# Performer attention: each head's product over its own 32 feature rows

## The reference

```python
q_kernel = jnp.exp(h_q + (proj_q - q_stab))         # q_stab = h_q
k_kernel = jnp.exp(h_k + (proj_k - k_stab))
q_prime = nc * (q_kernel + KERNEL_EPS)              # KERNEL_EPS = 1e-4
k_prime = nc * (k_kernel + KERNEL_EPS)
S = S + kt[..., :, None] * vt[..., None, :]         # a scan over the tokens
Z = Z + kt
num = jnp.einsum('bhm,bhmd->bhd', qt, S)            # m = 32 features
den = jnp.einsum('bhm,bhm->bh', qt, Z)
```

## Time and profile before

| | |
|---|---|
| median of 3 runs | 2310.37 us (2308.21 to 2314.17) |
| profiled execution | 2307.16 us, span 2305.4 us |
| PE busy | 2055.2 us, 89% |
| DVE busy | 1951.0 us, 85% |
| ACT busy | 1476.1 us, 64% |
| POOL busy | 948.3 us, 41% |
| mean granted TensorE clock | 0.958 |

### The profile page before, as it was taken

The page is one execution under the profiler, slowest core; times in us unless marked ns, Lnnn a source line. Parts: engine busy times, 40 slices in busy tenths (PEclk is TensorE's granted clock), DMA queues, the critical chain, the costliest instruction groups (busy, mean ns, idle before and its releaser), DMA issues. The chain is left out here.

```text
span 2305.4 us, 41495 instructions
## 1 busy us (share of the span) xinstructions
PE 2055.2 (89%) x12569; PEld 1606.9 (70%) x12569; DVE 1951.0 (85%) x7828; ACT 1476.1 (64%) x3637; POOL 948.3 (41%) x1374
## 2 busy tenths in 40 slices
PE   5879798989999899998999899898999899888677
PEld 3556577656986578766886579775887669767466
DVE  1289797998989898998989899898989989796982
ACT  3546367776676667686577667676677766468341
POOL 3232213554164534544155443544345541443441
PEclk9878889999999999999999999999999999899798
DMA  4000101000100101001100101001010001001000
GB/s 188 1 8 1 35 7 50 1 8 29 56 4 1 35 6 53 1 2 35 42 18 1 35 2 56 4 1 35 13 47 1 1 29 56 31 1 56 1 3 3
DMA packets 29503, 55.03 MB, mean 24 GB/s; under 512 B 2914, under 2 KB 10082, under 8 KB 28642
## 3 DMA queue, kind: packets, MB, share of 16 engines
q1 hardware_dynamic: 29282, 52.37, 7.0%
HBM read 51.31 MB, written 1.05 MB: 23 GB/s over the span
## 5 line engine op out<-in xcount | busy, mean ns | idle before, releaser
L265 DVE MATCH_REPLACE8 top_work<-top_eight,top_work 128x256 f32<-128x256 f32 x1664 | 666.9, 408 | 0.0
L267 DVE MAX8 top_eight<-top_work 128x8 f32<-128x256 f32 x1664 | 616.7, 412 | 0.2
L305 POOL TENSOR_TENSOR top_p<-top_p,top_rest 128x512 f32<-128x512 f32 x192 | 244.4, 1273 | 217.4 <-ACT top_rest L298 217.4
L850 PE MATMUL bank<-workP 128*128 128x256 f32 x1024 | 278.1, 396 | 9.1 <-POOL workP L1012 4.0
L990 ACT ACTIVATE att_pP<-bank,att_tinyP 128x256 f32<-128x256 f32 x512 | 215.2, 476 | 67.2 <-DVE att_tinyP L1039 66.4
L850 PEld LDWEIGHTS bank<-workP 128*128 128x128 f32 x1024 | 181.3, 194 | 55.7 <-issue 29.9
L1039 DVE TENSOR_REDUCE att_tinyP<-bank 128x2 f32<-128x512 f32 x256 | 172.6, 679 | 24.1 <-PE bank L850 23.0
L267 DVE MAX8 top_lead<-bank 128x8 f32<-128x256 f32 x384 | 144.6, 417 | 46.4 <-PE bank L645 22.7
L298 ACT ACTIVATE top_rest<-top_work,top_nmax 128x256 f32<-128x256 f32 x384 | 173.3, 503 | 10.6 <-DVE top_work L265 10.3
L273 POOL TENSOR_SCALAR top_nmax<-top_lead 128x2 f32<-128x2 f32 x192 | 37.5, 195 | 336.9 <-DVE top_lead L267 336.6
L1012 POOL TENSOR_SCALAR workP<-workP,const 128x256 f32<-128x256 f32 x256 | 122.3, 484 | 130.3 <-PE bank L850 94.4
(11 more groups left out here) (365 smaller groups left out, 4587.8 us busy)
## 6 DMA issues: line engine op xcount, KB each, us to landing
gelu_w<-in_pack3w SPq DMA_DIRECT2D x72, 256.0 KB, 3.0
top_qk<-in_pack3w SPq DMA_DIRECT2D x72, 256.0 KB, 2.8
pack<-in_pack SPq DMA_DIRECT2D x1, 4352.0 KB, 19.7
pack<-in_pack SPq DMA_DIRECT2D x1, 2266.0 KB, 9.8
pack<-in_pack SPq DMA_DIRECT2D x1, 1028.0 KB, 8.1
mix_wb<-in_ctx SPq DMA_DIRECT2D x1, 1024.0 KB, 4.9
x_in<-in_x SPq DMA_DIRECT2D x8, 128.0 KB, 2.1
ctx_tok<-in_ctx SPq DMA_DIRECT2D x8, 128.0 KB, 2.4
```

Source lines behind the costliest of these rows:

```text
L265: ins = nc.vector.match_replace(self.work[:, u % 2, j, :], eight, src, GONE)
L267: ins = nc.vector.max(eight, src)
L305: self.k.nc.gpsimd.tensor_tensor(v, v, self.rest[:, :, :], ALU.subtract).then_inc(*self.p_ready.one())
L850: mm = self.k.nc.tensor.matmul(self.banks[u % 2][:, j * T:(j + 1) * T], self.q1[:, u % self.RING, j * P:(j + 1) * P], self.kT, start=True, ...
```

## The change

The masked copies are gone, with their semaphore, ring and the two constants. The two products of a head take only the 32 partitions of its strip, of kf and of qf, as operands. The 1e-4 is added to qf by POOL, in two more instructions of the same form and size as for kf. The first head waits for the third of the four additions, the ninth for the fourth.

```diff
-            pe.wait_ge(*self.q1_ready.at(u + 1))
+            if u == H // 2:
+                pe.wait_ge(*self.kf_ready.at(4))
             if u >= 2:
                 pe.wait_ge(*self.a_copied.at(u - 1))
-            out, kf, q1 = b[u % 2], self.kf[:, u // HG, :], self.q1[:, u % self.RING, :]
-            nc.tensor.matmul(out[:, 0:T], kf[:, 0:P], q1, start=True, stop=True)
-            nc.tensor.matmul(out[:, T:T + P], kf[:, P:T], q1[:, P:T], start=True, stop=True).then_inc(*self.a_ps.one())
+            g, a = divmod(u, HG)
+            r = slice(PAD * a, PAD * (a + 1))
+            out, kf, qf = b[u % 2], self.kf[r, g, :], self.qf[r, g, :]
+            nc.tensor.matmul(out[:, 0:T], kf[:, 0:P], qf, start=True, stop=True)
+            nc.tensor.matmul(out[:, T:T + P], kf[:, P:T], qf[:, P:T], start=True, stop=True).then_inc(*self.a_ps.one())
...
-            act.wait_ge(*self.exp_ready.at(4))
-            for u in range(2):
-                self.act_q1(act, u)
-        u = self.at(s, 0, 0)
-        if u >= 0 and u + 2 < H:
-            self.act_q1(act, u + 2)
...
-            for half in range(2):
+            for half in range(4):
                 pool.wait_ge(*self.exp_ready.at(half + 1))
-                v = self.kf[:, 2 * half:2 * half + 2, :]
+                v = (self.kf, self.qf)[half // 2][:, 2 * (half % 2):2 * (half % 2) + 2, :]
                 nc.gpsimd.tensor_scalar(v, v, 1e-4, 1.0, ALU.add, ALU.mult).then_inc(*self.kf_ready.one())
```

More of the change, by code:

```diff
@@ L28 @@
 RF_SCALE = float(D) ** -0.25
-CONST = [("ident", 128), ("tri", 128), ("ones", 128), ("hsum", NG * 128), ("head_rows", H), ("group_rows", HG), ("group_eps", HG), ("part_rows", E16),
+CONST = [("ident", 128), ("tri", 128), ("ones", 128), ("hsum", NG * 128), ("head_rows", H), ("part_rows", E16),
          ("sim", E16), ("bq0", 1), ("bk0", 1), ("bq2", 1), ("bk2", 1), ("bq3", 1), ("bk3", 1)]
@@ L376 @@
 class Performer(Units):
-    RING = 4
     def __init__(self, k, side, x, ctxT, ctx_tok, banks, load, start=None):
@@ L386, in __init__ @@
         self.ksq = work.pT[:, 0, 0, :]
-        self.qf, self.kf, self.q1 = work.qT, work.kT, work.extra
+        self.qf, self.kf = work.qT, work.kT
         self.v = work.v
@@ L396, in __init__ @@
         self.proj_ready, self.exp_ready, self.kf_ready = k.sem(n + "proj"), k.sem(n + "exp"), k.sem(n + "kf")
-        self.q1_ready = k.sem(n + "q1")
         self.a_ps, self.a_copied, self.a_masked = k.sem(n + "a_ps"), k.sem(n + "a_copied"), k.sem(n + "a_masked")
@@ L432, in pe @@
             if u == 0:
-                pe.wait_ge(*self.kf_ready.at(2))
+                pe.wait_ge(*self.kf_ready.at(3))
                 pe.wait_ge(*self.exp_ready.at(4))
-            pe.wait_ge(*self.q1_ready.at(u + 1))
+            if u == H // 2:
+                pe.wait_ge(*self.kf_ready.at(4))
             if u >= 2:
                 pe.wait_ge(*self.a_copied.at(u - 1))
-            out, kf, q1 = b[u % 2], self.kf[:, u // HG, :], self.q1[:, u % self.RING, :]
-            nc.tensor.matmul(out[:, 0:T], kf[:, 0:P], q1, start=True, stop=True)
-            nc.tensor.matmul(out[:, T:T + P], kf[:, P:T], q1[:, P:T], start=True, stop=True).then_inc(*self.a_ps.one())
+            g, a = divmod(u, HG)
[3 more added lines that the diff above has]
+            nc.tensor.matmul(out[:, T:T + P], kf[:, P:T], qf[:, P:T], start=True, stop=True).then_inc(*self.a_ps.one())
         u = self.at(s, 3, 0)
@@ L490, in act @@
             nc.scalar.activation(self.oT[:, g, :], b[2][:, (g % 2) * T:(g % 2 + 1) * T], ACT.Copy).then_inc(*self.oT_copied.one())
[L492 to L499, removed]
     def pool(self, pool, s):
@@ L2739 @@
         "hsum": hsum.reshape(D, -1), "head_rows": np.kron(np.eye(H, dtype=f), np.ones((HD, 1), f)),
-        "group_rows": np.kron(np.eye(HG, dtype=f), np.ones((PAD, 1), f)),
-        "group_eps": np.kron(np.eye(HG, dtype=f), np.full((PAD, 1), 1e-4, f)),
         "part_rows": np.concatenate([np.tile(np.eye(E16, dtype=f), (PARTS, 1)), np.zeros((P - PARTS * E16, E16), f)]),
```

## The result

The changed kernel takes 2396.06 us (median of 5 runs, 2393.03 to 2397.28) where the one before takes 2310.01 (5 runs, 2308.21 to 2314.17): ratio 1.0366, interval 1.0352 to 1.038. The forecast was 2311 with a range of 2302 to 2319. It was wrong, and the case that came true is the rival that had a chance of 0.04: the granted clock falls to 1.2 GHz.

A forecast was written before the change was run, and what follows sets the result against it. Bounds: waits between engines in block 0, DVE in the second stretch, nearly full DVE and PE in six others. -2.0 + 0 + 2.8 + 0 = +0.8 on 2307.16 gives 2308.0, 2311 in median terms; range 2302 to 2319.

The forecast's parts named there:

- the last rival: Products of 32 rows drop the granted clock to 1.2 GHz: +8 at least from block 0, 2319 or above, chance 0.04.
- Part 2, the length of a product: Products over 32 rows keep their length: 0.215 us per 256-column pass, 0.107 per 128-column pass, 0.645 a head.
- neighbouring heads overlap: Faster rival: strips or free borders bring PE earlier in six stretches, DVE's waits go: -7.4 us, 2303, chance 0.24.
- Part 2, the borders: Switching between full and 32-row products costs 0.10 and 0.19 us; DVE's wait grows 0.81 to 1.28, six stretches +2.8.
- Part 1, block 0: Batch 0's stretch without masked copies: first L451 1.0 us earlier, two later distances 0.5 shorter each, -2.0 us in all.
- Part 3's 0 for block 0: POOL's two more additions cost nothing in block 0: the third ends at 27.35, ahead of ACT's 27.42.
- Part 1, second stretch: Removing masked copies gains nothing where DVE is busy 41.83 of 44 us: 0, between -0.3 and +0.5.
- Part 1, the six: In the six alike later stretches, removing copies lets PE come 0.5 us earlier, carried on to L645.
- C2: Experiments' theory, not the prediction's: overlap of neighbouring heads, with the idle time PE gets by it, lowers the clock.
- C1: Experiments' theory, not the prediction's: a product over 32 rows lowers the clock by its height alone.

The follow-up runs named there:

- full height: The changed kernel with each head's two products over all 128 rows again, masked copies still gone: 2318.09 us, ratio 1.0034.
- 64 rows: The changed kernel with each head's products over its own strip and the neighbour's: 2327.2 us, ratio 1.0074.
- one strip for all: The changed kernel with every head's products over rows 0 to 31 of its group, so neighbours can't overlap: 2341.44 us, ratio 1.0142.
- the additions alone: The kernel before, with two more POOL additions that add 0 to kf and a wait for them: 2312.63 us, ratio 0.9997.
- the last run: The kernel before, with the query copies and masks of block 0 moved to DVE: 2312.45 us, ratio 1.0002.
- short masks: POOL's masks cut to 32 of 128 columns, on the changed kernel with products over 128 rows: 2294.11 us; on the changed kernel with its strips: 2329.23 us.
- one by one: The changed kernel, where a head's products wait until those of the head before have ended on PE: 2380.7 us, ratio 1.0284.

## Why the prediction was wrong

**The step that failed** is the clock's term. The sum has none: Part 2 takes the length of a product "as unchanged", at 0.215 us a pass, and the clock stands only in the last rival, set aside by "Against: nothing in the rows ties it to the height of an operand". The forecast took the absence of a row as evidence, and gave 0.04. The runs showed some 81 us there, worked out below, and 78 that go when the height alone is put back. Its price, "+8 at least" from block 0 alone, was near for block 0 (44.1 for 35.6, +8.5, of which 1.3 is the late rise of the clock ahead of the heads) and left out the other seven. What the clock took can be told from the rest: with each stretch at the time that a related kernel reached near or at the full clock (34.6 for block 0, from full height; 43.1 for the second; 42.9 and 5 x 43.4 for the six, from 64 rows), the sum would be 337.6, or 6.5 over before. The other 81.3 of the 87.8 us are the clock's and its waits'. That is worked out between kernels and not measured by itself.

**Part 2, the length of a product, "I take as unchanged"**, failed in two ways. At full clock the pair of heads is shorter (0.86 us, not 1.29). The rival that "neighbouring heads overlap" was right in its mechanism. The Trainium skill (TensorE: Matmul & The Clock Gate, Part 3: Packing small matmuls) has matmuls in different tiles of the array run concurrently. The trace agrees as far as 0.86 for 1.29. But it saves some 0.45 us a pair at full clock, PE stands idle for 1.97 us in front of yM in the same stretch, and at 1.2 GHz it is far outweighed: A's pass of 256 columns has its median at 479 ns, before 379.

```profile
L438 PE MATMUL bank<-workP x256: 373/479/792, 28.9 to 1835.6; 32*128 32x256 f32 x128
```

**Part 2, the borders**, was near. The prices of 0.10 and 0.19 together, 0.29, meet the 0.19 by which a pair of heads becomes longer (1.50 for 1.31) plus 0.09 ahead of it (the first pass starts 0.20 us after the pass before it, where 0.11 is usual at full height). The wait at L1769 is 1.40 for 1.28 forecast. That a stretch is +0.5 over full height, for +0.47 forecast over before, is in part luck: L358 gave back 0.7 there, and the borders and what hangs on them took 1.2, not 0.97. At 32 rows without overlap the five stretches that hold the clock (one strip for all) take the same, 42.8 and 43.4.

**Part 1, block 0**, was right: -2.0 forecast, and -2.4 at full height when both are taken from the start of the copy L373 on (26.9 us for 29.4). The stretch as a whole shows only -1.0, since in that profile its first projections ran at the lower clock. In the prediction's own steps: the first L450 came at 32.73, and less the 1.34 us by which everything ahead of it was late, that is 31.4 for a forecast of 31.6; its followers come after 2.35 and 2.62 us in turn, for 2.4 and 2.6. Part 3's 0 for block 0 was right too. The load of the first product ends its wait of 1.15 us on the third addition, but ACT's last exp ends at 28.77 in the same place, 0.1 before the product starts.

**Part 1, second stretch**: 0 forecast, "DVE has no wait to lose". Full height is 1.1 us shorter, and the additions alone are 1.1 longer. Neither is proof against the step: the last run has this stretch 1.0 longer with the program of before in it, so such differences come without an edit. Why full height is shorter was not followed.

**Part 1, the six**: "the lead is carried". The wait at L1769 fell from 0.81 to 0.20 in the three short stretches of full height, and also with short masks, where L358 holds DVE up far less; so PE's lead is a likely cause, though it was not measured by itself. But the stretches are 0.9 us longer, not shorter. Without the copies POOL's work comes at other times and meets the two L358; the additions alone don't bring this about. In the kernel before the place looks as follows (timeline of the fourth stretch; for the end of the chain see the full-height rows above):

```profile
670.92 1.27 POOL L519 TENSOR_TENSOR att_pTP<-att_pTP,const 128x512 f32<-128x512 f32 x1 [0.87 <-ACT att_pTP L485]
672.11 0.77 DVE L358 TENSOR_SCALAR yM<-x,ln_mvM,ln_rstdM 128x128 f32<-128x128 f32 x2
672.33 0.48 POOL L713 TENSOR_SCALAR top_qk<-top_qk,const 128x256 f32<-128x256 f32 x1
672.77 1.27 POOL L305 TENSOR_TENSOR top_p<-top_p,top_rest 128x512 f32<-128x512 f32 x1
```

DVE goes between POOL's two long instructions, beside short ones, in 0.77 us. At full height L358 starts 0.24 us after L305 and takes 2.33: +1.5 on the engine that bounds the stretch, less 0.6 from the wait, is +0.9, and 42.9 against 42.0 is what is measured. The Trainium skill (SBUF — State Buffer, Who interferes with whom) says that a tensor_scalar of DVE can take the ports that it shares with GpSimd, and that the one that comes first holds them for its whole instruction. The traces agree for POOL first: each time the pair ends 0.08 to 0.09 us after POOL's second instruction, and takes 2.33 us. POOL held up by DVE is not shown by any row here. The prediction did not ask what POOL would be doing when L358 comes.

**The clock, as far as it is settled.** Shown: the loss is bound to the low products (full height holds 0.96 or more in the six, with nearly the same idle time before yM); the height alone can do it, at 32 rows (one by one; one strip for all) and in block 0 at 64 rows, also ahead of any idle time for yM; and work at full height between the strips holds it in all six, where one by one, which has no overlap either, loses it in three. C2 alone is refuted by one by one. C1 alone, by which a low product always takes the clock, is refuted by five held stretches of one strip for all.

Argued, not shown: that idle time before yM makes a lapse likelier or longer. For it: every lapse of the twelve alike stretches begins within 2.4 us of that place, and with short masks the six take 46.2 to 41.5 us for 57.8 to 48.6. Against: the short masks moved more than the idle time, and some lapses come ahead of yM. Open: why, with the same instructions, one stretch holds the clock and the next loses it, and why a later fall lasts longer. In block 0 and the second no kernel with low products and nothing beside them was found that keeps the clock of before, but for the second at 64 rows (43.1 us, 0.85).

## What to carry to other kernels

Before an operand is cut to fewer rows, ask what the clock will do, not only whether a pass gets longer: on a nearly full PE, 16 heads over 32 rows cost 8.5 us in block 0 and 7 to 16 in each later stretch. A mask or zero rows that keep the product at full height can be cheaper than the strip. And where work is taken off one engine, read which instructions of POOL and DVE come to lie beside each other afterwards: a pair of L358 that took 0.77 us came to take 2.33 without an edit of its own. Where a difference of a microsecond in one stretch matters, compare from the same instruction on, and look for it in a run whose program is unchanged there: the late rise of the clock put 1.1 to 1.3 us into block 0 of some profiles and not of others.

## What the runs showed of the hardware that was not expected

- The granted clock fell from 1.00 to 0.50 with PE busy 3.94 of each 4 us (one by one, 968 to 976), and was at 0.50 for 32 us with PE busy 4.00 of 4 (changed kernel, 711 to 743). A busy PE in the profile is thus no sign of a held clock.
- One more full-height product of 128 columns for each head made the six stretches shorter (47.1 us for a mean of 53.1).
- Heads in neighbouring strips overlap in fp32: eight passes of A and B per pair in 0.86 us, for 1.31 at full height and 1.50 if both take the same strip.
- Shortening POOL's masks to a quarter gave 24.0 us at full height (2318.09 to 2294.11), though POOL is busy only 41% of the span. In the stretches that hold the clock in both, four DVE instructions beside POOL's masks account for it.
